# At most two scatters of target scores in flight, in the five edge-weight stages of a graph network kernel

## The reference, cut to what matters

```python
xW = (x @ W).reshape(n, heads, out_ch)
alpha_s = jnp.sum(xW * a_src, axis=-1)
alpha_d = jnp.sum(xW * a_dst, axis=-1)
e = jax.nn.leaky_relu(alpha_s[src] + alpha_d[dst], SLOPE)
m = jax.ops.segment_max(e, dst, num_segments=n)
w = jnp.exp(e - m[dst])
z = jax.ops.segment_sum(w, dst, num_segments=n)
alpha = w / z[dst]
out = jax.ops.segment_sum(xW[src] * alpha[:, :, None], dst, num_segments=n)
```

## Time and profile before

| | us |
|---|---|
| median of 3 runs | 10321.53 |
| lowest and highest | 10313.65, 10325.05 |
| the profiled execution's own time | 10293.34 |
| its span, first to last instruction | 10291.6 |

### The profile page before, as it was taken

One profiled execution on the slowest core, in us unless ns is written; L12 is line 12 of the kernel. 1 busy time (PEld: TensorE's weight loads), 2 busy tenths in 40 slices (PEclk: granted clock), 3 DMA queues, 4 the chain that ended last, 5 costly groups with the idle time before them and its releaser, 6 DMA issues. The chain is left out here.

```text
span 10291.6 us, 89481 instructions
## 1 busy us (share of the span) xinstructions
PE 6457.9 (63%) x25974; PEld 4026.9 (39%) x25974; DVE 5072.5 (49%) x10547; ACT 2679.0 (26%) x6047; POOL 3711.5 (36%) x3723
## 2 busy tenths in 40 slices
PE   6847455797477545469964553654853677537756
PEld 6723233343455323247743232332442333213334
DVE  7831465222777543621056554446563888543121
ACT  0122000222444123112224431321232555212211
POOL 2626465001366256220044744650121555110111
PEclk5579666899699766679977765666876899768868
DMA  4200233101366233114433324330030222210012
GB/s 108 62 6 10 78 92 78 38 28 39 112 178 179 74 108 90 43 56 164 149 84 94 91 66 127 92 78 2 15 105 28 68 68 67 69 46 8 7 62 78
DMA packets 440685, 758.49 MB, mean 74 GB/s; under 512 B 172573, under 2 KB 268795, under 8 KB 437521
## 3 DMA queue, kind: packets, MB, share of 16 engines
q0 software_dynamic: 182080, 437.26, 15.7%
q1 hardware_dynamic: 239987, 295.32, 9.1%
q10 hardware_dynamic: 18136, 20.19, 0.6%
HBM read 669.59 MB, written 82.56 MB: 73 GB/s over the span
## 5 line engine op out<-in xcount | busy, mean ns | idle before, releaser
L2456 POOL DMA_INDIRECT R<-table,edges x1248 | 1242.0, 995 | 813.8 <-issue 292.9
L2508 DVE TENSOR_TENSOR acc<-acc,PS 125x256 f32 (+3 forms) x1664 | 704.7, 423 | 1206.5 <-PE PS L2525 506.1
L2525 PE MATMUL PS<-R,hot 128*125 128x256 f32 (+1 forms) x1664 | 690.7, 555 | 490.3 <-issue 313.4
L2525 PEld LDWEIGHTS PS<-R,hot 128*125 128x125 f32 x1664 | 383.4, 261 | 797.5 <-issue 635.9
L2468 ACT ACTIVATE R<-R,TW 128x128 f32<-128x128 f32 (+1 forms) x1248 | 494.0, 431 | 672.9 <-DMA R<-table,edges 631.3
L2276 PE MATMUL PS<-S,hotT 125*128 125x100 bf16 (+1 forms) x6240 | 364.1, 219 | 474.7 <-DVE hotT L2383 399.7
L2523 PE MATMUL PS<-R,hot 128*125 128x258 f32 x1664 | 446.3, 420 | 193.1 <-DVE acc L2506 116.3
L2456 POOL DMA_INDIRECT xx<-table,edges x416 | 414.9, 997 | 380.9 <-PE PS L2525 308.1
L2456 POOL DMA_INDIRECT room<-table,edges x416 | 427.8, 1028 | 297.2 <-PE PS L2525 124.5
L2276 PEld LDWEIGHTS PS<-S,hotT 125*128 125x128 bf16 x6240 | 316.4, 113 | 523.1 <-DVE hotT L2383 364.8
L1759 POOL DMA_INDIRECT sorted_edges<-edge_rows,edge_place x391 | 399.5, 1022 | 321.7 <-DVE edge_place L1997 113.5
(11 more groups left out here) (718 smaller groups left out, 13360.8 us busy)
## 6 DMA issues: line engine op xcount, KB each, us to landing
rowb<-slo_row SPq DMA_DIRECT2D x260, 250.0 KB
W<-in_L_ffn_W1p SPq DMA_DIRECT2D x32, 1024.0 KB
W<-in_L_ffn_W2p SPq DMA_DIRECT2D x32, 1024.0 KB
near<-dst_row SPq DMA_DIRECT2D x98, 256.0 KB
R<-table,edges POOLq DMA_INDIRECT x1248
W<-in_L_ffn_w SPq DMA_DIRECT2D x16, 1024.0 KB
hib<-hi_mask SPq DMA_DIRECT2D x260, 50.0 KB
g<-gate_rows POOLq DMA_DIRECT2D x8, 1568.0 KB
```

Of the source, the lines that this page charges most:

```text
L2456: pool.indirect_dma_start(self.R[:, u, 0:self.W], None, self.table[:, :], bass.IndirectOffsetOnAxis(ap=self.G.edges[:, g, 0:1], axis=0)).t ...
L2508: v.tensor_tensor(to, to, self.G.PS[0:P, self.bank + k, 0:self.WH], ALU.add).then_inc(self.put, 1)
L2525: mm = pe.matmul(self.G.PS[0:P, self.bank + k, 0:self.WH], hot, self.R[:, u, :], start=True, stop=True)
```

## The change

The 25 scatters of a weight stage now count on two semaphores by turns (`dmoved[0]` for even ones, `dmoved[1]` for odd ones). Before each scatter from the third on, POOL waits until the last but one has landed. The wait ahead of the `d0` gathers becomes one for each of the two semaphores. This holds for all five stages. Nothing else is changed.

```diff
-        hot_odd = s.sem("hot_odd")
-        split, hot, gathered, taken, summed, steps, dmoved, dgot, ...
+        hot_odd, dmoved = s.sem("hot_odd"), [s.sem(f"dmoved{j}") for j in range(2)]
+        split, hot, gathered, taken, summed, steps, dgot, ...
...
                 for t in range(T):
+                    if t >= 2:
+                        pool.wait_ge(dmoved[t % 2], 16 * (t // 2))
                     pool.indirect_dma_start(fill[:, :], bass.IndirectOffsetOnAxis(ap=G.first_at[:, t:t + 1], axis=0),
-                                            AL[:, t, H:2 * H], None).then_inc(dmoved, 16)
-                pool.wait_ge(dmoved, 16 * T)
+                                            AL[:, t, H:2 * H], None).then_inc(dmoved[t % 2], 16)
+                for j in range(2):
+                    pool.wait_ge(dmoved[j], 16 * len(range(j, T, 2)))
                 for g in range(CT):
```

More of the change, by code:

```diff
@@ L2206, in edge_weights @@
         far, apart = s.sb("far", [P, 512], BF16) if H > 1 else None, s.sem("apart")
-        hot_odd = s.sem("hot_odd")
-        split, hot, gathered, taken, summed, steps, dmoved, dgot, dload, zturned, tail, ready, rows_done, exp_done, back, out = [
-            s.sem(x) for x in ("split", "hot", "gathered", "taken", "summed", "steps", "dmoved", "dgot", "dload", "zturned", "tail",
+        hot_odd, dmoved = s.sem("hot_odd"), [s.sem(f"dmoved{j}") for j in range(2)]
+        split, hot, gathered, taken, summed, steps, dgot, dload, zturned, tail, ready, rows_done, exp_done, back, out = [
+            s.sem(x) for x in ("split", "hot", "gathered", "taken", "summed", "steps", "dgot", "dload", "zturned", "tail",
                                "ready", "rows", "exp", "back", "out")]
```

## The result

| | kernel before | changed kernel |
|---|---|---|
| median of 18 runs, us | 10303.2 (10286.0 to 10325.1) | 10337.4 (10315.0 to 10367.9) |
| ratio, 95% interval | | 1.0030 (1.0021 to 1.0039) |
| span of the profiled execution, us | 10291.6 | 10336.9 |
| the same kernels once more (e12), medians, us | 9874.7 | 9960.7, ratio 1.0094 (1.0079 to 1.0108) |

The prediction was 10327, and 10337.4 lies within its range of 10284 to 10346. Part of that is luck. The prediction stood on a median of three runs, 10321.5; with 18 runs the kernel before has 10303.2. The predicted change was +5.4 us, in stage 2 alone; the measured one is +34.3 us (0.3%), six times as much, and put on 10321.5 it would have given 10356, outside the range. Where e12 ran, the same change costs 0.94%, three times as much. What follows is about that.

What follows compares the result with a forecast made beforehand. No engine was near full; POOL held only stage 2's barrier, 5.2 us beyond the other engines. Its later end cost 5.4 us there, 0 elsewhere: 10327 us on the 10321.5 median, range 10284 to 10346.

Steps and rivals of the forecast that it cites:

- The landing time: POOL's scatters: landing 2.62 us behind the issue, so one each 1.90 us, making POOL 9.4 us later a stage.
- The early gathers' 2.84 us: POOL's early gathers beside row loads step 2.84 us; taken as upper end for the scatters, POOL then 31 us late.
- The d0 wait on two semaphores: POOL ahead of the d0 gathers: one wait more, taken as nothing, at most 1.5 us over five stages.
- The scans: DVE's first scan: 14.9 us to spare in stage 2, 18 in stage 1; the 9.4 us delay hidden in all five.
- POOL's end: Barriers behind the early gathers: stage 2 pays 5.4 us, stage 4 hides it in 9.0 us to spare, others nothing.
- The source side, taken as zero: DVE's products beside the scatters: pace unchanged, 0 us, since cost per scatter is fixed and number in flight hardly changes.
- a fixed 0.60 us a scatter: Source side beside scatters: 15.1 us lost over 25 scatters, the same however they are spaced.
- the number in flight: Scatters: 2.6 in flight on average before, 2.0 after, so the waits take little of a crowd away.
- Both rivals: Crowding was the cause (-48 us, chance 0.20), and the slow stretch or slow landings (21 us or more later, chance 0.14).
- Crowding: Source side returns to its later pace beside the scatters: -48 us in all, 10274; chance 0.20.
- landings at 2.84 us with scans that wait: POOL 31 us late, scans wait 13 us in stages 1, 3, 5: 10387; chance 0.14 shared with a longer slow stretch.

Runs made afterwards that it cites:

- e12: The changed kernel as it is, run once more against the kernel before: 9960.7 against 9874.7 us, ratio 1.0094.
- e10: The changed kernel without its 23 waits a stage, only the two semaphores left, against the kernel before: ratio 0.9996.
- e13: The kernel before with three early gathers in flight instead of two: ratio 1.0003.
- e15: The kernel before with one POOL memset between scatters, first scan 16 groups later, three early gathers in flight: ratio 0.9945, 10240.4 against 10309.0 us.
- e16: The kernel before with two POOL memsets between scatters, first scan 16 groups later, three early gathers in flight: ratio 0.9951.
- e2: The kernel before with only the first scan of each stage put 16 groups later: ratio 1.0000.
- e11: The kernel before with four early gathers in flight instead of two: ratio 0.9995.
- e3: The changed kernel with four scatters in flight instead of two (four semaphores), against the kernel before: ratio 1.0001.
- e14: The changed kernel with SP's row and mask loads held back until all 25 scatters of a stage have landed: 10431 us in a single execution.

## Why the prediction was right in the number and wrong in the sum

**The landing time is the step that failed.** "How long a landing takes" was read from the wait ahead of the d0 gathers, 2.62 us behind the end of the last issue, 3.8 us from its start. That it was the last landing of a batch is not the fault: in e10 the same wait is 21.9 / 5 = 4.4 us, 5.6 us from the start, no less than the median landing of 5.3 us there. The fault is the traffic beside it: the source side ran at little more than half pace then, with 93 to 98 GB/s in all. The same wait is 13.9 / 5 = 2.8 us in e13, beside 91 to 97 GB/s, and 22.5 / 5 = 4.5 us in e15, beside 131 to 136, both in the 10300 group. The change itself brought the traffic to 132 to 139 GB/s, and beside that a landing takes 5.1 us (e12). The prediction took the two terms one by one, the landing and the source side, and each moved the other. The step was 2.5 to 2.6 us and not 1.90, and POOL was 25 to 28 us late by stage and not 9.4. The early gathers' 2.84 us, which I had as the upper end, was nearer to the truth than 1.90: the same rule, beside loads at their later pace.

**The d0 wait on two semaphores** costs nothing: right (e10).

**The scans** had 14.9 and 18 us to spare by a generous bound, and that was right against 9.4. Against 27 it isn't, and the source side came to the scan sooner. They waited 18.4 to 21.4 us.

**POOL's end**: the mechanism was right, its size not. 27.5 us late instead of 9.4 at 5.4 / 9.4 gives 15.8; stage 2 paid 14.2. Stage 4 used up its 9.0 us and paid 7.1.

**The source side, taken as zero, was wrong in the 10300 group.** 13 to 15 products in 31 us became 23 and 24. Both reasons for the zero failed. The cost isn't a fixed 0.60 us a scatter: e15 and e16 issue the same 25 and make 23 and 24 products. And the number in flight says little: e10 has 5.3 / 1.49 = 3.6 in flight, more than the 2.6 that the prediction worked out for the kernel before, and its source side isn't slowed. e15 shows that neither landing waits nor a cap are needed: 1.82 us a step instead of 1.49 frees it.

**Both rivals came true at once.** Crowding, priced at -48 us, and landings at 2.84 us with scans that wait, priced at +66: together 10321.5 + 18 = 10339.5. Measured: 10337.4. That these agree to 2 us is luck again, since 10321.5 is 18 us too high; the change itself is +34.3 and not +18. I had treated them as exclusive. In the 9870 group only the second exists, and the change costs 0.94%.

What stays open: why the source side is slowed by a scatter each 1.49 us in the 10300 group (10 stages of 10 in two traces, the kernel before and e13) and not in the 9870 group (15 of 15 in e2, e10 and e11, and 5 of 5 in e3, whose step is 1.52 to 1.62). No run turns the one into the other, and the chip's number doesn't tell them apart. It isn't the granted clock alone, since stage 2 has 0.50 in both. And e15 has three edits; that its source pace comes from the memset follows from e13 (three gathers, 13 and 14 products), but the later scan wasn't run by itself in the 10300 group, and no trace of dense scatters was kept from e15's own comparison.

## What to carry to other kernels

A cap on transfers in flight makes a step of the landing time divided by the cap. Read the landing time from the start of the issue, beside the traffic that it will have once the change is in; if the change speeds that traffic up, the landing gets longer. Measure the kernel before often enough: three runs were 18 us off here, more than three times the predicted change. If transfers slow another stream, space them by a little idle time of the issuing engine before you make it wait for landings: 0.33 us a scatter freed here what 27 us of waiting a stage had freed. A gain on one side shows only if its next consumer isn't late: move the consumer in the same edit. And when two rivals work on different resources, price them together too.

## What was not expected

- The same kernel takes 10300 us in one group of comparisons and 9870 in the other, and the same change costs 0.3% in the first and 0.9% in the second. The chip numbered 15 is in both groups. An interval of 0.1% to either side holds for the comparison that it was measured in.
- Beside the row loads a scatter of 125 rows lands 5.1 to 5.3 us from the start of its issue; with the source side held back it lands within 3.0 us (e14).
- The scatters slow the exchange between DVE and PE, neither of which has a part in them: beside them, in the 10300 group, its groups came each 2.1 to 2.4 us (31 / 15 to 31 / 13), at 1.82 us a scatter and more each 1.3 (31 / 24 and 31 / 23). From a `hotT` to its product it is 3.9 to 4.0 us instead of mostly 1.4 to 2.1 (e10). The low clock of stages 1 and 5 comes with it (0.50 in e13, 0.81 in e15's stage 1).
